# Two-layer graph network: layer 0 multiplies node rows by the message weights before the sum over edges, with counts stationary

## What is computed

```python
# layer 0
msg = (x[src] + rel_emb[edge_type]) @ W_msg.T + b_msg
agg = segment_sum(msg, dst) / max(deg, 1)
x1  = layernorm(x + x @ W_self.T + b_self + agg)
# layers 1 and 2
h   = swish(mean(x1[src]) @ W1_l.T + b1 + x1 @ W1_r.T)
out = layernorm(x1 + mean(h[src]) @ W2_l.T + b2 + h @ W2_r.T)
```

## Time and profile before

| | |
|---|---|
| median of 3 runs | 340.17 us (339.83 to 340.46) |
| the profiled execution: time, span of its core | 339.44 us, 337.6 us |
| PE busy | 323.0 us, 96% of the span |
| DVE, ACT busy | 69%, 51% |
| groups counted in | 11.4 to 164 us |
| layers 1 and 2 | from about 177 us |

### The profile page before, as it was taken

The page is one execution under the profiler, slowest core; times in us unless marked ns, Lnnn a source line. Parts: engine busy times, 40 slices in busy tenths (PEclk is TensorE's granted clock), DMA queues, the critical chain, the costliest instruction groups (busy, mean ns, idle before and its releaser), DMA issues.

```text
span 337.6 us, 9130 instructions
## 1 busy us (share of the span) xinstructions
PE 323.0 (96%) x3288; PEld 239.1 (71%) x3288; DVE 232.7 (69%) x611; ACT 170.7 (51%) x376; POOL 4.6 (1%) x18
## 2 busy tenths in 40 slices
PE   5699999999999999999999998999999999999993
PEld 2588899999999999999994545545555545545663
DVE  6999999998998999999347887034136255155154
ACT  3597787879779779879512413212214212211212
POOL 5000000000000000000000000000000000000000
PEclk9879999999999999999999999999999999999998
DMA  4702000000000000000211111111001112220111
GB/s 127 269 23 76 2 2 3 10 2 4 8 2 4 8 5 5 6 2 2 79 29 31 24 25 19 26 24 27 6 16 30 24 27 53 59 51 22 37 43 36
DMA packets 22654, 10.53 MB, mean 31 GB/s; under 512 B 16349, under 2 KB 21584, under 8 KB 22608
## 3 DMA queue, kind: packets, MB, share of 16 engines
q1 hardware_dynamic: 22320, 9.48, 11.3%
q10 hardware_dynamic: 288, 0.43, 0.5%
HBM read 4.75 MB, written 1.60 MB: 19 GB/s over the span
## 4 chain that ended last, share of the span: by engine, by line
PE 79%; DVE 12%; ACT 3%; issue 2%; ACTq 0%; DVEq 0%
PE ps L1099 31%; PE ps L1080 19%; PE ps L1023 17%; PE ps L1150 5%; PE ps L1170 3%; DVE hot L1333 2%; DVE hot L1326 2%; PE ps L1030 1%; DVE table L1343 1%; PE ps L1040 1%; DVE peaks L1569 1%; ACT counts L964 1%; ACT scaled L905 1%; PE ps L1128 1%; ACT table L949 0%
## 5 line engine op out<-in xcount | busy, mean ns | idle before, releaser
L1099 PE MATMUL ps<-counts,table 128*128 128x512 f16 (+3 forms) x785 | 134.0, 329 | 0.0
L964 ACT CAST counts<-ps 128x494 f32 x208 | 107.5, 580 | 30.4 <-PE ps L1023 29.7
L1099 PEld LDWEIGHTS ps<-counts,table 128*128 128x128 f16 x785 | 63.9, 97 | 65.2 <-DVE table L1475 0.5
L1080 PE MATMUL ps<-counts,table 128*128 128x256 f16 x600 | 80.0, 271 | 0.3 <-ACT sum_first L890 0.3
L1023 PE MATMUL ps<-hot 128*128 128x143 f16 (+1 forms) x592 | 65.5, 236 | 3.6 <-DVE hot L1333 3.1
L1023 PEld LDWEIGHTS ps<-hot 128*128 128x128 f16 x592 | 52.0, 102 | 6.7 <-DVE hot L1333 4.9
L1080 PEld LDWEIGHTS ps<-counts,table 128*128 128x128 f16 x600 | 52.0, 96 | 5.6 <-issue 0.4
L1333 DVE TENSOR_TENSOR hot<-iota,edges 128x1100 f16<-128x1100 f16 x74 | 53.6, 724 | 0.0
L1326 DVE TENSOR_TENSOR hot<-iota,edge_rows 128x768 f16<-128x768 f16 x74 | 40.7, 551 | 2.9 <-PE ps L1060 2.8
L1030 PE MATMUL ps<-window_hot,hot 128*128 128x19 f16 x296 | 41.7, 180 | 0.0
L905 ACT ACTIVATE scaled<-ps,rdeg 128x128 f32<-128x128 f32 (+1 forms) x75 | 21.8, 373 | 24.1 <-PE ps L1150 21.7
(11 more groups left out here) (146 smaller groups left out, 322.7 us busy)
## 6 DMA issues: line engine op xcount, KB each, us to landing
own_T<-x_turned SPq DMA_DIRECT2D x4, 256.0 KB, 2.7
edge_rows<-table SPq DMA_TRANSPOSE x54, 2.4
table<-x_rows SPq DMA_DIRECT2D x1, 832.0 KB, 6.0
table<-x_rows SPq DMA_DIRECT2D x1, 768.0 KB, 4.3
out<-new_first SPq DMA_DIRECT2D x3, 256.0 KB, 2.5
sum_first<-x_turned SPq DMA_DIRECT2D x2, 256.0 KB, 4.8
out<-hot SPq DMA_DIRECT2D x2, 256.0 KB
window_hot<-table SPq DMA_TRANSPOSE x23, 2.4
```

What stands on the lines that cost most here:

```text
L964: nc.scalar.copy(A[:, HALVES[half], bass.ds(bases[group % 8], GROUP_W)], window(group, half)).then_inc(copied[half], 1)
L1080: last = nc.tensor.matmul(ps[:, sums_bank(q), at:at + PART], table0[:, b, which, :], A[:, b, part * PART:(part + 1) * PART], start=k == at ...
L1099: last = nc.tensor.matmul(ps[:, sums_bank(q), 0:nodes], table[:, b, which, :], A[:, b, at:at + nodes], start=b == which == 0, stop=b + 1 = ...
```

## The change

Layer 0 is reordered. The node rows (and the relation embeddings) are loaded transposed and multiplied once by the message weights (`project`, fp32, 25 matmul tiles in groups 1 to 9); ACT and DVE split the products into the two fp16 parts of the table, out of PSUM. The biases are added to the 64 relation rows, which every edge picks exactly once (`bias_relations`). In the aggregation the counts are now stationary (128 x 128) and the table rows move, 128 columns a matmul, in *tiles* of 128 nodes; the result stands in rows of nodes, so `scale` reads it from PSUM directly. `lead` and `messages` are gone for chunks 0 to 5. Chunk 6 keeps the old form, with an identity matrix for the message weights. Own products of chunks 0 to 4 come in groups 10, 12, 13, 15, 18, without `bias_own`. The third buffer of one-hots is there from the start. The reduce over the table and the degrees of chunks 5 and 6 move ahead of the end of chunk 4 on DVE.

```diff
-PART = 256
-EARLY_PARTS = 11
-BIASED = (5, 7, 9, 15)
-OWN = (7, 9, 11, 18)
+EARLY_TILES = 23
+PROJECTED = (1, 2, 3, 5, 6, 8, 9)
+OWN = (10, 12, 13, 15, 18)
 # spread()
-        room = 0 if group in OWN else 6 + group % 2
+        room = 0 if group in OWN + PROJECTED else 13
-        if part < EARLY_PARTS and group > READY[part]:
+        if tile < EARLY_TILES and group > max(READY[tile], PROJECTED[-1]):
 # SyncE
-            for half, span in enumerate((slice(0, cut), slice(cut, BLOCKS))):
-                sp.dma_start(stage_x[:, span, :].rearrange("p b d -> p (b d)"),
-                             x_rows[:, span.start * D:span.stop * D]).then_inc(x_in[half], 16)
+            sp.dma_start(weights_first[:, 0, :], w_msg).then_inc(message_weights_in, 16)
+            cut = CHUNKS // 2 * CHUNK
+            for half, span in enumerate((slice(0, cut), slice(cut, BLOCKS * P))):
+                sp.dma_start(stage[:, span], x_turned[:, span]).then_inc(x_in[half], 16)
 # ScalarE
+            def high_bits(c):
+                act.wait_ge(projected_done, c + 1)
+                if c == CHUNKS - 1:
+                    act.wait_ge(relations_biased, 2)
+                nc.scalar.activation(
+                    table0[:, projected_blocks(c), 0, :],
+                    projected(c).rearrange("p (b d) -> p b d", d=D), ACT.Copy, scale=SCALE
+                ).then_inc(x_hi, 1)
 # TensorE
+            def project(c):
+                ...
+                for t in range(tiles.stop - tiles.start):
+                    first = c * CHUNK + t * P
+                    last = nc.tensor.matmul(projected(c)[:, t * P:(t + 1) * P],
+                                            stage[:, first:first + P], weight(0, 0),
+                                            start=True, stop=True)
 # aggregate_part -> aggregate_tile
-                        ps[:, sums_bank(q), at:at + PART], table0[:, b, which, :],
-                        A[:, b, part * PART:(part + 1) * PART], start=k == at == 0,
+                        ps[:, sums_bank(q), at:at + P], A[:, b, tile * P:(tile + 1) * P],
+                        table0[:, b, which, :], start=k == at == 0,
 # VectorE
+                if group - LOW_LATE in PROJECTED:
+                    low_bits(PROJECTED.index(group - LOW_LATE))
+                if group == PROJECTED[-1] + 1:
+                    bias_relations()
...
+                    if q == EARLY - 1:
+                        check_table()
+                        degrees(EARLY)
+                        degrees(EARLY + 1)
```

More of the change, by code:

```diff
@@ L85, with products_of @@
-UNREAD = 15
-LOW_PIECES = ((16, 19), (19, 22), (22, 25), (0, 4), (4, 8), (8, 12), (12, 16))
-LOW_FROM = 10
-LOW_LATE = 3
[L94 to L100, removed]
+PROJECTED = (1, 2, 3, 5, 6, 8, 9)
+PROJECTED_BANKS = (4, 5, 6, 7)
+LOW_LATE = 3
+OWN = (10, 12, 13, 15, 18)
+OWN_BANKS = (7, 6, 7, 6, 6)
+UNREAD = 18
+def products_of(tile):
+    if tile:
         return [(b, which) for b in range(BLOCKS) for which in range(2)]
-    return [(b, 0) for b in range(BLOCKS)] + [
-        (b, 1) for first, end in LOW_PIECES for b in range(first, end)]
+    return [(b, which) for which in range(2) for b in range(BLOCKS)]
@@ L106, in spread @@
 def spread():
-    products, done, tiles = [], [0] * EARLY, [[0] * SUB for _ in range(EARLY)]
-    part, at, waiting = 0, 0, []
+    products, done = [], [0] * EARLY
+    tile, at = 0, 0
     for group in range(GROUPS):
-        room = 0 if group in OWN else 6 + group % 2
[L113 to L117, removed]
+        room = 0 if group in OWN + PROJECTED else 13
@@ L118, in spread @@
         first, count = at, 0
-        if part < EARLY_PARTS and group > READY[part]:
-            count = min(max(room, 0), 2 * BLOCKS - at)
-        products.append((part, first, first + count))
+        if tile < EARLY_TILES and group > max(READY[tile], PROJECTED[-1]):
+            count = min(room, 2 * BLOCKS - at)
+        products.append((tile, first, first + count))
         at += count
         if at == 2 * BLOCKS:
[L124 to L138, removed]
+            if tile % SUB == SUB - 1:
+                done[tile // SUB] = group
+            tile, at = tile + 1, 0
+    return products, done, (tile, at)
+BEHIND, DONE, LEFT = spread()
 MOST_EDGES = 2048.0
@@ L990, in _ @@
                 ahead = CHUNKS <= q and not short(q)
-                if not ahead:
+                if q > EARLY and late(q - 1) <= 0:
+                    scale(q - 1)
+                if q > EARLY and not ahead:
                     lead(q)
-                if q > EARLY:
+                if late(q - 1) > 0:
                     scale(q - 1)
@@ L1133, in dense @@
             def dense(q, tiles):
-                messages(q, tiles)
-                if q >= POSTED:
-                    own_later(q, tiles)
+                if late(q) > 0:
+                    messages(q, tiles)
+                own_later(q, tiles)
             def messages(q, tiles):
@@ L1169, in own_later @@
                     to = ps[0:size, dense_bank(q), t * D:(t + 1) * D]
-                    last = nc.tensor.matmul(to, x_T(q)[:, at], weight(layer, 1), start=False,
-                                            stop=False, skip_group_check=True)
+                    last = nc.tensor.matmul(to, x_T(q)[:, at], weight(layer, 1),
+                                            start=q == EARLY and t == 0, stop=False,
+                                            skip_group_check=True)
                 if t + 1 == tiles_of(q):
```

354 lines of the change are left out of this document (164 added, 190 removed).

## The result

The changed kernel takes **336.2 us** (median of 4 runs, 335.55 to 336.81); the kernel before took 340.12 beside it (4 runs, 339.83 to 340.46). The ratio is 0.9877, 95% interval 0.9858 to 0.9896: faster by 1.2%. The forecast was 335.3 us in a range of 333.4 to 338.8; its direction and its range held. The profiled execution took 336.58 us with a span of 334.8; its counterpart before had 339.44 and 337.6. So the two profiles differ by 2.8 us where the medians differ by 3.9.

A forecast was written before the change was run, and what follows sets the result against it. PE, 96% busy, was taken as the bound, with DVE deciding the first stage. +0.25 to group 19, +0.4 in the loop and -5.5 behind it sum to -4.85 us: 335.3 us in the median's terms, range 333.4 to 338.8.

The forecast's parts named there:

- rival B: Loop: 128-column matmuls run slower than 0.056 us; no gain from 0.060, 346 us at 0.065; chance 0.09.
- The loop: Group 19 to the last count's end: 122.6 us becomes 123.0, +0.4 us (0 to +1.5).
- the loss at chunk ends: Loop: 2.6 us lost around the ends of five chunks; 1.5 kept, as `scale` still delays copies PE waits for.
- To group 19: Stretch up to group 19's start: moves from 41.35 to 41.6 us, +0.25 us.
- rival A: Start and chunk ends: half clock stays until 20.7 us and no chunk-end loss returns; 337.8 us, chance 0.15.
- the walk: Up to group 19: DVE and PE followed group by group at trace prices; PE the bound from group 12, at 30.5.
- Behind the loop: After the last count: fewer matmuls, no chunk 5 messages, one wait gone, one new; -5.5 us.
- a new wait of 0.5: Layer 1's first sweep: PE wants block 24 at T+18.9, chunk 6's table rows come at T+19.4; T: last count's end.
- The 1.0 goes: At the checks: PE's 1.0 us wait for chunk 8's sums vanishes because the reduce has moved away.
- the messages' term: PE drops message products: 24 tiles including chunk 4's own product, 5.4 us in the loop; chunk 5's 0.97 behind it.
- Rival D: Chunks late: DVE bounds the loop or chunk 4's longer way delays the sweep; 337.3 us at 2 us; chance 0.08.
- rival C: Loop: PE's sequencer loads places while queued matmuls run out, +4.3 us, 339.6; chance 0.08 together with no effect.

The follow-up runs named there:

- e7: Changed kernel with ACT's `scale` of a chunk split into two tiles each behind two groups' copies; 333.64 us, ratio 0.9813.
- e9: Kernel before the change with `scale` of chunks 0 to 3 split into two tiles each in two groups; 338.54 us, ratio 0.9951.
- e6: Changed kernel with 6 instead of 18 unread warm-up matmuls ahead of the first group; 338.17 us, ratio 0.9946.
- e10: Changed kernel with each of the 1200 128-column matmuls of layer 0's aggregation issued as two of 64 columns; 349.99 us, ratio 1.0281.
- e1: Changed kernel with the two copies of stacked counts issued amid chunk 7's eight transposed loads, not behind them; 334.94 us, ratio 0.9843.
- e2: Changed kernel with the reduce over the table moved back behind the checks of the edges; 335.99 us, ratio 0.9878.
- e4: Changed kernel with 24 unread fp32 matmul tiles added on PE, as many as `messages` had for chunks 0 to 5; 340.23 us, ratio 0.9987.
- e3: Changed kernel with the third buffer of one-hots used only from group 14 on, as before; 336.99 us, ratio 0.9904.

## Why the prediction was right, and where its steps were off

- **The price of 0.056 us for 128 columns with new weights** held between counts too: 0.0554. That decided the sign, and rival B fell. The 81 ns of the Trainium skill ("TensorE: Matmul & The Clock Gate", section Back-to-back issue gap) are met by no stretch here. The same section's formula for an isolated matmul at the upper clock level, N / 2.4 + 2.5 ns, gives by estimate 55.8 ns for 128 columns and 29.2 for 64, and the rows, which are of streams, have 55.4 and 28.8: the measurement decides.
- **The loop**: forecast 123.0 from group 19 to the last count's end, measured 165.40 - 42.18 = 123.2. That the loss at chunk ends is ACT's `scale` was an assumption; e7 shows it for 2.2 us in the changed kernel. I had kept 1.5 of 2.6. e9 adds that, by the loop of its profile, only about 0.9 of the old 2.6 were `scale`'s, so the new form pays more for it; why was not tested.
- **To group 19**: forecast +0.25, measured +0.83. The direction of the clock was right: it stayed at the upper level, where I had it back at 17 us, in the profiles of the changed kernel and of all its variants but e6. So rival A fell with its condition. What kept it up was not tested. The step that failed is the walk. Group 12 began at 30.79 for 30.5, since its one-hots were ready at 30.65 for 30.4, and the counts of groups 12 and 18 took 0.84 and 0.95 us for 0.73. At group 18 the load of places lies at 39.5 to 40.1 and the 11 matmuls from 39.64 last only 0.61: the row of e10 in small. That this is the cause there was read, not tested, and groups 10 and 11 have counts of 0.91 and 0.94 too.
- **Behind the loop**: forecast -5.5, measured 35.41 - 39.47 = -4.06. The 100 matmuls, the dropped messages (T+8.13 for T+7.95) and the table rows of chunks 5 and 6 (T+15.5 and T+19.0 for T+16.0 and T+19.4) came as worked out. The step that failed is "a new wait of 0.5", for `low` of chunk 6. There was none, and in its place one of 1.77 us that I had not looked for. I had costed the DMAs at nothing and not walked SyncE's queue behind the loop, though PE was to arrive there five microseconds earlier. e1 shows it. PE came to block 24 4.6 us earlier and the copies 0.8 later, against a cover of 3.6: that makes 1.8.
- **"The 1.0 goes"** was right with a wrong cause. I gave it to the reduce's move; e2 shows that it goes without. By the traces it went with `lead`, and I had costed `lead` at nothing. That this term came out right is luck.
- **The sum**: +0.83, +0.59 in the loop, -4.06, -0.16 after it make -2.80 for my -4.85. In profiles the change gained 58% of what I had forecast. The median was 0.9 us over the forecast and not 2.0, because the profiled execution before lay under its median and the one after over its own; that the forecast came so close is luck too. e4 confirms the messages' term: 24 tiles at the forecast's 0.23 are 5.5 us, and put back they cost 5.3 to 5.6.

Rival D's late chunks and rival C's sequencer did not decide. C's condition is near: e10 meets it. The argument that I had against C, that PE idled only 0.5 of 124 us, was worth nothing, since e10 loses 0.3 us at each load and its rows show PE idle for only 0.4 us of the same window. What speaks against C is that thirteen matmuls with a load among them take no longer than thirteen without.

## What to carry to other kernels

When an engine is made to reach a stage earlier, walk every queue that feeds the stage at its new time, the queue of DMA issues too: a transfer that was covered by some 3.6 us became a wait of 1.8, and moving two lines took it away. A wait that vanishes has a cause of its own; undo the suspected edit before you credit it. On an engine that is 50% busy a block of 1.1 us can still cost the critical engine 2 us in all, if the critical engine's turnaround passes through it; cutting the block in two was the cheapest gain here.

## What the runs showed of the hardware that I had not expected

- A transposed load of 128 x 128 fp16 from SBUF holds SyncE's queue for 1.23 us, and in each profile one of the eight for longer, 1.51 to 2.33. Behind eight of them two copies, of 53.0 and 5.5 KB, release PE 4.64 to 4.66 us after the second one's issue, in all six profiles where PE waits for them. The wait was 1.77, 1.35, 1.24, 1.14, 0.97 and 0.76 us in the changed kernel, e10, e6, e2, e7 and e3, and in the changed kernel, e2 and e3 it goes with the second copy's issue, at T+16.5, 15.8 and 15.4.
- A stream of matmuls with new weights runs at 0.0554 us for 128 columns and 0.029 for 64. With a register load of 0.59 us in the sequencer among them, 13 of 128 columns lose nothing, while 26 of 64 columns, which take as long, lose 0.3 us with the count behind them, and the profile shows almost no idle time for it.
